# Layer 3 of a four-layer graph kernel: the leaky relu's maximum moved into VectorE's sum, and the exponential taken tile by tile with s2 as its bias

## The reference, cut to what matters

```python
def _L3_gnn_ref(h, adj_matrix, W, a):
    Wh = jnp.einsum('bnf,fo->bno', h, W)
    s1 = Wh @ a1
    s2 = Wh @ a2
    e = s1[:, :, None] + s2[:, None, :]
    e = jnp.where(e >= 0, e, 0.2 * e)
    e = jnp.where(adj_matrix[None] == 0, -jnp.inf, e)
    attention = jax.nn.softmax(e, axis=-1)
    return jnp.einsum('bij,bjo->bio', attention, Wh)
x = _layernorm(x + _L3_gnn_ref(x, adj, L3_gnn_W, L3_gnn_a), axis=-1)
```

## Time and profile before

| | |
|---|---|
| median of 3 runs | 1164.62 us (1164.52 to 1164.92) |
| span of the profiled execution | 1163.7 us |
| around the span, by the median | 0.9 us |
| layer 3 in the trace | from about 983 us to the end |
| TensorE busy | 1002.3 us, 86% |
| VectorE busy | 727.6 us, 63% |
| ScalarE busy | 450.3 us, 39% |
| GpSimd busy | 198.0 us, 17% |

### The profile page before, as it was taken

How to read it: one execution, slowest core, us unless ns; L and a number is a source line. 1 busy time by engine, 2 the same in 40 slices (tenths; PEclk the granted TensorE clock), 3 DMA queues, 4 the chain that set the end, 5 groups by cost and what they waited for, 6 DMA issues and landing times. The chain is left out here.

```text
span 1163.7 us, 19102 instructions
## 1 busy us (share of the span) xinstructions
PE 1002.3 (86%) x5486; PEld 681.5 (59%) x5532; DVE 727.6 (63%) x2226; ACT 450.3 (39%) x734; POOL 198.0 (17%) x266
## 2 busy tenths in 40 slices
PE   3969999999997697926899999999999995899995
PEld 2748999999997586413444444444444442566663
DVE  7853455554454565635667767777777642688885
ACT  2111121121120265710444444544544442577762
POOL 5000110111100000050011111111111001155554
PEclk7879999999998899955799999999999998899998
DMA  6000000000000000004222222222223200000001
GB/s 185 1 28 19 10 19 19 10 18 18 9 0 1 9 0 0 0 8 108 55 56 55 54 54 54 54 58 64 66 60 68 66 1 3 1 27 27 27 27 37
DMA packets 32629, 40.07 MB, mean 34 GB/s; under 512 B 6352, under 2 KB 15696, under 8 KB 32592
## 3 DMA queue, kind: packets, MB, share of 16 engines
q1 hardware_dynamic: 32592, 39.61, 13.9%
HBM read 5.91 MB, written 4.19 MB: 9 GB/s over the span
## 5 line engine op out<-in xcount | busy, mean ns | idle before, releaser
L1221 DVE CUSTOM_DVE_ANT_0 junk<-bank,mask_ij 128x512 bf16<-128x512 f32 x256 | 170.7, 689 | 80.7 <-PE bank L1306 75.6
L1160 ACT ACTIVATE prob<-wide 128x1024 f32<-128x1024 f32 x128 | 128.0, 1024 | 44.5 <-PE wide L1320 44.1
L1306 PE MATMUL bank<-qk_st 96*128 96x512 f32 x256 | 122.2, 517 | 25.3 <-DVE mx L1221 15.8
L1319 PE MATMUL wide<-qk_st 128*128 128x512 f32 x256 | 116.2, 523 | 0.3 <-ACT prob L1160 0.3
L596 ACT CAST yT<-wide 128x512 fp32r<-128x512 f32 x48 | 28.1, 586 | 217.6 <-PE wide L699 162.7
L505 POOL TENSOR_SCALAR n_rstd<-n_aggr 128x4 f32<-128x4 f32 x64 | 12.6, 198 | 506.7 <-DVE n_aggr L498 494.6
L1306 PEld LDWEIGHTS bank<-qk_st 96*128 96x128 f32 x256 | 49.2, 201 | 82.5 <-DVE mx L1221 37.4
L1320 PE MATMUL wide<-mask_ji,identb 128*128 128x512 bf16 x226 | 88.8, 393 | 0.0
L58 PE MATMUL bank<-z,L3T_hi 128*128 128x256 f32 x256 | 73.8, 288 | 6.3 <-DVE z L657 6.3
L1633 PEld LDWEIGHTS bank<-Wh,pr 128*128 128x128 f32 x512 | 61.1, 196 | 23.8 <-issue 19.9
L1633 PE MATMUL bank<-Wh,pr 128*128 128x129 f32 x512 | 65.3, 282 | 10.9 <-ACT pr L1501 10.9
(11 more groups left out here) (256 smaller groups left out, 2273.3 us busy)
## 6 DMA issues: line engine op xcount, KB each, us to landing
qk_st<-qkT SPq DMA_DIRECT2D x192, 128.0 KB, 2.4
Xf<-X SPq DMA_DIRECT2D x16, 256.0 KB, 2.3
out_dram<-rc SPq DMA_DIRECT2D x16, 256.0 KB, 2.3
A<-in_adj_dram SPq DMA_DIRECT2D x1, 1024.0 KB, 5.5
w<-in_L_gnn_W_dram SPq DMA_DIRECT2D x2, 128.0 KB, 2.3
qk_st<-neg_row SPq DMA_DIRECT2D x16, 8.0 KB, 1.8
W<-in_L_gnn_W_dram SPq DMA_DIRECT2D x1, 192.0 KB, 2.4
w_sb<-in_L_gnn_w_dram SPq DMA_DIRECT2D x1, 64.0 KB, 5.0
```

The costliest lines, as they stand in the source:

```text
L1160: act.activation(flat(prob[jp][h][:]), wide[k % 2][:], ACT.Exp, scale=SCALE).then_inc(t_exp, 1)
L1221: dve.tensor_tensor_reduce(out=junk[k % 2][:], in0=src[:], in1=m.mask_ij[:, k % NT], scale=1.0, scalar=3.0 * MASKED, op0=ALU.add, op1=ALU.max,
L1306: pe.matmul(out[:], q_st[bp][0:3 * HD, h, i * P:i * P + P], k_st[bp][0:3 * HD, h], start=True, stop=True).then_inc(s_ps, 1)
L1319: pe.matmul(ps, k_st[bp][:, h, j * P:j * P + P], q_st[bp][:, h], start=True, stop=False)
```

## The change

What is added before the exponential is written another way: relu(0.8 (s1+s2)) + 0.2 s2 = max(0.8 s1, -0.8 s2) + s2. ScalarE copies 0.8 s1 once per batch into `s1r` (letter l, now once in `ORDER`); VectorE's instruction at e takes the maximum of it with -0.8 s2 and adds the bank; ScalarE's exponential adds s2 as its bias, which is another number in each of the four tiles, so there are four exponentials of 512 columns where there were two of 1024.

```diff
-        for what in "a a x a a d r r d r r e e w w e e j i E E b m B m m l m c l c l l g c".split():
+        for what in "a a x a a d r r d r r e e w w e e j i E E b m B m m l m c c g c".split():
...
                     elif what == "l":
-                        if k == 0:
-                            act.wait_ge(s1_ps, after(s, 1))
-                            act.wait_ge(ss, after(s, 2))
-                            act.wait_ge(e_s, after(s - 2, NT))
-                        act.activation(rl[par][:, k], bank[1][:], ACT.Relu, scale=1.0 - SLOPE,
-                                       bias=s2s[par][:, 0, k:k + 1]).then_inc(relu, 1)
+                        act.wait_ge(s1_ps, after(s, 1))
+                        act.wait_ge(e_s, after(s - 2, NT))
+                        act.activation(s1r[par][:], bank[1][:], ACT.Copy, scale=1.0 - SLOPE).then_inc(s1_c, 1)
...
                     elif what == "E":
-                        act.wait_ge(e_s, after(b, NT, 2 * k + 2))
-                        two = flat(pr[1 - par][:, 2 * k:2 * k + 2])
-                        act.activation(two, two, ACT.Exp).then_inc(ex, 1)
+                        for t in (2 * k, 2 * k + 1):
+                            act.wait_ge(e_s, after(b, NT, t + 1))
+                            act.activation(pr[1 - par][:, t], pr[1 - par][:, t], ACT.Exp,
+                                           bias=s2s[1 - par][:, 1, t:t + 1]).then_inc(ex, 1)
...
-                            dve.wait_ge(relu, after(s - 2, NT))
-                            for n, f in enumerate((1.0 - SLOPE, SLOPE)):
+                            dve.wait_ge(ex, after(s - 2, NT))
+                            for n, f in enumerate((SLOPE - 1.0, 1.0)):
...
                     elif what == "e":
                         if k == 0:
                             dve.wait_ge(av, after(b - 2, NT))
-                        dve.wait_ge(relu, after(b, NT, k + 1))
+                        dve.wait_ge(ss, after(b, 2))
+                        dve.wait_ge(s1_c, after(b, 1))
                         dve.wait_ge(r_ps, after(b, NT, k + 1))
-                        dve.scalar_tensor_tensor(out=pr[1 - par][:, k], in0=bank[4 + k % 2][:],
-                                                 scalar=s2s[1 - par][:, 1, k:k + 1], in1=rl[1 - par][:, k],
-                                                 op0=ALU.add, op1=ALU.add).then_inc(e_s, 1)
+                        dve.scalar_tensor_tensor(out=pr[1 - par][:, k], in0=s1r[1 - par][:],
+                                                 scalar=s2s[1 - par][:, 0, k:k + 1], in1=bank[4 + k % 2][:],
+                                                 op0=ALU.max, op1=ALU.add).then_inc(e_s, 1)
...
                     elif what == "i":
-                        pe.wait_ge(relu, after(s - 1, NT))
+                        pe.wait_ge(s1_c, after(s - 1, 1))
                         pe.matmul(bank[1][:], wB[0][:], xT[par][:], start=True, stop=True).then_inc(s1_ps, 1)
                     elif what == "a":
                         h, t = divmod(k, 2)
-                        pe.wait_ge(ex, after(b, 2))
+                        pe.wait_ge(ex, after(b, NT))
```

More of the change, by code:

```diff
@@ L1382, in layer3 @@
         dg = [sb(f"dg{k}", [P, NT, P], BF16) for k in range(2)]
-        rl = [sb(f"rl{k}", [P, NT, N]) for k in range(2)]
+        s1r = [sb(f"s1r{k}", [P, N]) for k in range(2)]
         pr = [sb(f"pr{k}", [P, NT, N]) for k in range(2)]
@@ L1398, in layer3 @@
         d_g = sem("diagonals")
-        relu = sem("relu")
+        s1_c = sem("s1_rows_out")
         r_ps = sem("mask_and_rows"); e_s = sem("e_summed")
@@ L1465, in _ @@
             act.sem_inc(x_c, CREDIT)
-            act.sem_inc(ex, CREDIT * 2)
+            act.sem_inc(ex, CREDIT * NT)
             act.sem_inc(wh_c, CREDIT * 2)
-            act.sem_inc(relu, CREDIT * NT)
+            act.sem_inc(s1_c, CREDIT)
             act.sem_inc(d_g, CREDIT * NT)
```

## The result

| | before | changed |
|---|---|---|
| median | 1164.57 us (6 runs) | 1168.68 us (6 runs) |
| lowest to highest | 1163.8 to 1166.19 | 1167.29 to 1169.57 |
| span of the profiled execution | 1163.7 us | 1167.6 us |

The ratio is 1.0036, with a 95% interval of 1.0026 to 1.0047: slower by 0.36%. Measured once more beside the last experiment it was 1.0037 (1.0024 to 1.0049). The forecast was 1168.5. The interval means 3.0 to 5.5 us, so the medians alone can't tell a change of 3.5 us from one of 4.

What follows compares the result with a forecast made beforehand. A loop through TensorE, VectorE and ScalarE bounds the 9.53 us step, with no ScalarE slack from the copy of Wh through the exponentials. 4.8 + 0.08 - 0.62 - 0.35 = +3.9 on 1164.6 gives 1168.5 us, range 1165.8 to 1171.0.

Steps and rivals of the forecast that it cites:

- The exponentials, 2.57 us for 2.20, from a bias of 97 ns each: Layer 3 steps on ScalarE: four biased exponentials fill 2.57 us where two filled 2.20, +0.37 us per step.
- They start where they started, because the copy of Wh stands in front: ScalarE in the steady steps: the first exponential still starts at T + 2.91, T being the end of TensorE's a matmuls.
- Thirteen steps pay, the one before the last finds cover: Steps 2 to 14 pay 0.37 us each, +4.8 us; behind step 15 TensorE's 0.83 us wait absorbs it, 0.
- the shorter last piece: Step 16: ScalarE waits for the last sum, then the last piece takes 0.715 us for 1.06, -0.35 us.
- The relus are worth 0.62 us once and nothing else: Removing ScalarE's relus starts step 0's diagonals sooner, -0.62 us once; worth nothing in the steady steps.
- The term for step 1: Step 1: the exponentials start at the same point and four would end at 1005.38 for 1005.30, +0.08 us.
- The sum on VectorE costs nothing: VectorE's sum with the maximum keeps its 745 ns and the residual covers the two added sequencer instructions: 0.
- The exponentials cost less: Rival: four exponentials run at the relus' pace, +1.7 us, 1166.3; no change by the measurement, chance 0.13.
- The exponentials keep up with the sums: Rival: each exponential starts as its sum ends, -5.9 us, 1158.7; chance 0.05 with any other gain over 0.2%.
- The clock stayed at 1.00: Against the rival that TensorE's clock falls in the steady steps, 23 us more, 1191, chance 0.02.
- The idle time in front of the second reciprocal: Sign in the trace: VectorE's wait before the second reciprocal grows from 0.60 to about 0.97 us.

Runs made afterwards that it cites:

- the last experiment: Kernel before with four unbiased exponentials, the first two in front of the copy of Wh, and the two scalings of s2 moved from VectorE to ScalarE: 1161.81 us, ratio 0.9979.
- the direct pair of experiments: Kernel before with four exponentials of 512 columns, first without an operand per partition (1161.57 us), then with a scale read per partition (1168.49 us).
- the one letter moved: Changed kernel with letter E moved, so a step's first two exponentials stand in front of the copy of Wh (letter w): 1160.73 us, ratio 0.9974.
- the kernel with the old sum: Kernel before, relus and old sum kept, with four exponentials of 512 columns, each reading a scale of ones per partition: 1168.49 us, ratio 1.0034.

## Why the prediction was right

The prediction named the loop, the place and the price, and each was found:

- *The exponentials, 2.57 us for 2.20, from a bias of 97 ns each.* They take 717 ns in the median and fill 2.56 us. The step is 9.90 us, as given. Luck had a part in so close a hit: the price per operand is 89 ns by the direct pair of experiments, 8 less than I took, and the exponential without one takes 630 ns, 12 more than the cast of 618 from which I built it. And the 0.37 us per step are not the bias alone, as I would have read them: four times 0.09 us are the bias, some 0.17 us are the split, by the estimate above, and a like amount came back because ScalarE no longer waits for the last sum. Only the four times 0.09 were measured by themselves.
- *They start where they started, because the copy of Wh stands in front.* Shown by the trace (2.04 us behind the first sum in both) and by the one letter moved: the step of 9.90 us becomes 9.47.
- *Thirteen steps pay, the one before the last finds cover.* From the first start of a to that of step 16 the time grew from 1138.78 - 1005.44 = 133.34 to 1143.56 - 1005.09 = 138.47 us, by 5.13: fourteen times 0.37, the fourteenth being that of step 15, which then finds its cover. Step 16 then gives back 0.82 us (9.33 becomes 1152.07 - 1143.56 = 8.51), which holds the 0.37 of cover and the 0.35 of the shorter last piece, and 0.1 more.
- *The relus are worth 0.62 us once and nothing else.* The first start of a came 0.35 us sooner although layer 3 began 0.42 us later in this execution, so 0.77 us were gained up to there, for -0.62 + 0.08 = -0.54 in the sum. The diagonals of step 0 account for 0.62 of it exactly (997.53 - 985.70 becomes 997.33 - 986.12). The term for step 1 was wrong in sign, by a little: I had the exponentials start at the same point, and they started 0.26 us sooner still, so that step 1 gave 0.15 us where I had it cost 0.08. In the steady steps they are worth nothing (9.46 with them, 9.47 without, the letter moved in both).
- *The sum on VectorE costs nothing.* About 0.02 us per step in the changed kernel, by the kernel with the old sum. Behind two exponentials, where the last sum is on the path, 0.07 us appeared. As a statement on the change the step holds; as one on the sum by itself it was too smooth.
- *The rivals.* "The exponentials cost less" fell with 717 ns, and the last block's clock did not stay up in the changed kernel. "The exponentials keep up with the sums" fell, as ScalarE started them at 1051.89, 0.72 us behind the copy of s. The clock stayed at 1.00 from 1020 to 1140 us. What page "ScalarE: Activation LUTs" of the Trainium skill advises in "Rules for kernel authors", relu and max on VectorE, did nothing for this kernel: ScalarE's time was saved where it was idle.

Three things in the text were loose. First, VectorE does not wait for TensorE in front of each second reciprocal: in one step of two it arrives just with it. Before the first reciprocal of that step 0.49 us pass for which the profile names no releaser. It is the place where the loop of two unrolled steps begins anew, so I take it for the branch. Two rows of the kernel before, then two of the changed one:

```profile
1046.90 0.17 DVE L1570 RECIPROCAL rec<-bank 128x2 f32<-128x2 f32 x1 [0.49 <-issue]
...
1047.89 0.17 DVE L1570 RECIPROCAL rec<-bank 128x2 f32<-128x2 f32 x1
```

```profile
1046.99 0.16 DVE L1564 SCALAR_TENSOR_TENSOR em<-s,em 128x4 f32<-128x4 f32 x1
1047.64 0.17 DVE L1569 RECIPROCAL rec<-bank 128x2 f32<-128x2 f32 x1 [0.49 <-issue]
```

It did no harm to the forecast, in which VectorE only gained slack, but it is the likely reason why I expected 9.3 us from the moved letter and got 9.47: VectorE had less room than I read from one row. The idle time in front of the second reciprocal, for which I gave 0.97 us, came to 0.85 in one step and 0.31 in the other.

Second, the runs lie some 1.9 us above their own spans (1169.57 with a span of 1167.6), not 0.9. With 1.9 us around it the span of 1163.7 would give 1165.6, which is none of the three runs of before, so the 0.9 lay between the median and the span of another execution. It did no harm: the forecast is the median of before plus the change, whatever lies around the span.

Third, the total was hit more closely than its terms. From its first matmul on, layer 3 grew by 3.5 us, not 3.9: -0.77 at the start, +5.13 in the steps, -0.82 in step 16 and -0.06 behind it. The medians moved by 4.1, with an interval of 3.0 to 5.5, so that 1168.5 against 1168.68 is closer than the measurement can vouch for. What stands by itself is the step: 9.53 to 9.90 us.

## What to carry to other kernels

Read what stands in front of an instruction in its engine's queue before splitting it: here four exponentials could use none of their earlier inputs, because a copy that waited for later data stood ahead of them. An operand read per partition had its price in each instruction here (0.09 us at 512 columns; other lengths were not tried), so a fusion that buys it with more and smaller instructions pays it each time; if that engine is in the loop, fusing can lose what it saves elsewhere. Time saved in front of an idle stretch is worth nothing, and once the bound is moved, the next one may be a few hundredths of a microsecond away.

## What the runs showed of the hardware

An exponential of 512 columns takes 630 ns without an operand per partition and about 720 with one, whether it is the scale (719) or the bias (720); with both it takes 810. Behind one another four fill 2.20 us without one and 2.56 with one.

The last 32 matmuls of the program take either 5.3 to 5.5 us or 3.84 us. The windows view, first of the changed kernel and then of the four exponentials without an operand:

```profile
1150.00:1152.00 2.00, 0.38 (x2) 0.00 (x0) 2.00 (x6) 1.76 (x3) 0.00 (x0) 1.00 0.37 103
1152.00:1154.00 2.00, 1.93 (x12) 1.93 (x13) 0.42 (x5) 0.02 (x1) 1.15 (x2) 0.70 0.00 0
1154.00:1156.00 2.00, 2.00 (x11) 2.00 (x11) 0.69 (x3) 0.00 (x0) 1.79 (x4) 0.50 0.00 0
```

```profile
1145.40:1147.00 1.60, 0.05 (x1) 0.00 (x0) 1.60 (x6) 1.26 (x2) 0.00 (x0) 1.00 0.20 55
1147.00:1149.00 2.00, 1.98 (x17) 1.98 (x18) 0.47 (x5) 0.00 (x0) 1.11 (x2) 1.00 0.03 8
1149.00:1151.00 2.00, 1.86 (x17) 1.67 (x15) 0.88 (x4) 0.00 (x0) 1.79 (x4) 1.00 0.00 0
```

In one the granted clock falls to 0.50 (1.2 GHz) within the block, in the other it stays at 1.00 (2.4 GHz). TensorE stood idle for 1.69 us in front of it in the changed kernel and for 1.58 in the other; but the changed kernel with the letter moved had 1.69 as well and kept the clock, and the kernel with the scalings on ScalarE had 1.57 and lost it. The length of the pause alone does not decide it, and what does is open. It is worth 1.6 us, as much as four steps of the loss studied here. There is one trace of each kernel (two of the changed one, 5.48 us in both), so whether the other executions of a kernel have the same last block is not shown, and medians that lie closer than 1.6 us say little of the steps.
